# Quaternion sums as three 256-element instructions, with the memory's real part negated and the keys in another order

## The reference, cut to what matters

```python
def quat_mul(q1, q2):
    r1, i1, j1, k1 = (q1[..., 0], q1[..., 1], q1[..., 2], q1[..., 3])
    r2, i2, j2, k2 = (q2[..., 0], q2[..., 1], q2[..., 2], q2[..., 3])
    r = r1 * r2 - i1 * i2 - j1 * j2 - k1 * k2
    i = r1 * i2 + i1 * r2 + j1 * k2 - k1 * j2
    j = r1 * j2 - i1 * k2 + j1 * r2 + k1 * i2
    k = r1 * k2 + i1 * j2 - j1 * i2 + k1 * r2
    return jnp.stack([r, i, j, k], axis=-1)

keys = (x @ Wk.T + bk).reshape(B, L, N_QUAT, 4)        # 64 quaternions per token
keys = keys / jnp.maximum(norm(keys), NORM_EPS)
values = (x @ Wv.T + bv).reshape(B, L, N_QUAT, 4)
memory = jnp.cumsum(quat_mul(values, keys), axis=1)
retrieved = quat_mul(memory, quat_conj(keys)).reshape(B, L, D)
retrieved = retrieved / jnp.sqrt(positions)[None, :, None]
normed = layernorm(retrieved) * ln_g + ln_b
return x + (normed @ Wo.T + bo)
```

## Time and profile before

| | us |
|---|---|
| median of 3 runs | 720.98 |
| profiled execution | 720.35 |
| its span | 718.6 |
| busy PE | 652.3 (91%) |
| busy DVE | 613.9 (85%) |
| busy POOL | 569.9 (79%) |
| busy ACT | 414.1 (58%) |

### The profile page before, as it was taken

How to read it: one execution, slowest core, us unless ns; L and a number is a source line. 1 busy time by engine, 2 the same in 40 slices (tenths; PEclk the granted TensorE clock), 3 DMA queues, 4 the chain that set the end, 5 groups by cost and what they waited for, 6 DMA issues and landing times. The chain is left out here.

```text
span 718.6 us, 13029 instructions
## 1 busy us (share of the span) xinstructions
PE 652.3 (91%) x3536; PEld 541.8 (75%) x3536; DVE 613.9 (85%) x1378; ACT 414.1 (58%) x743; POOL 569.9 (79%) x879
## 2 busy tenths in 40 slices
PE   2999999999778988988988989989967999999997
PEld 2899998898556766766766766767756898999986
DVE  5878877765699999999999999999995877788764
ACT  4667777665435455454454454554526776677762
POOL 3788889875578888888888888888883689888873
PEclk9999999999989999999999999999988999999999
DMA  7720000000000000000000000000000011111112
GB/s 256 240 63 0 0 0 0 0 1 1 0 2 0 1 0 0 0 0 0 0 0 0 0 0 0 0 0 0 2 1 0 25 36 58 58 58 58 37 51 89
DMA packets 18442, 18.67 MB, mean 26 GB/s; under 512 B 752, under 2 KB 18160, under 8 KB 18416
## 3 DMA queue, kind: packets, MB, share of 16 engines
q1 hardware_dynamic: 18416, 18.36, 7.8%
HBM read 9.97 MB, written 8.39 MB: 26 GB/s over the span
## 5 line engine op out<-in xcount | busy, mean ns | idle before, releaser
L222 POOL TENSOR_TENSOR bhalf<-xn 128x128 f32<-128x128 f32 x256 | 118.1, 492 | 30.0 <-DVE xn L567 30.0
L1135 PE MATMUL bank<-wkv,m_xnT 128*128 128x256 f32 x512 | 134.9, 394 | 5.5 <-DVE khat L561 4.1
L1079 PE MATMUL bank<-wffn,kact 128*128 128x256 f32 x512 | 117.0, 381 | 1.6 <-DVE kact L402 1.6
L1135 PEld LDWEIGHTS bank<-wkv,m_xnT 128*128 128x128 f32 x512 | 92.2, 196 | 25.3 <-issue 4.5
L1079 PEld LDWEIGHTS bank<-wffn,kact 128*128 128x128 f32 x512 | 94.7, 190 | 13.9 <-issue 1.1
L284 POOL TENSOR_TENSOR xk_lo<-xk,xk_hi 128x1024 fp32r<-128x1024 f32 x30 | 71.0, 2368 | 31.9 <-ACT xk_hi L712 31.9
L946 POOL TENSOR_TENSOR xr_lo<-xr,xr_hi 128x1024 fp32r<-128x1024 f32 x32 | 76.2, 2381 | 18.1 <-ACT xr_hi L718 16.4
L953 POOL TENSOR_TENSOR res<-res,gating_buffers 128x1024 f32 (+1 forms) x31 | 75.4, 2433 | 9.1 <-DVE gating_buffers L409 8.6
L567 DVE TENSOR_TENSOR xn<-bank,khat 128x1024 f32<-128x1024 f32 x64 | 77.8, 1216 | 1.4
L567 DVE TENSOR_TENSOR gating_buffers<-bank,khat 128x1024 f32<-128x1024 f32 x64 | 77.6, 1212 | 0.0
L1046 PE MATMUL bank<-wffn_hi,xr_hi 128*128 128x256 f32 x256 | 71.4, 279 | 0.3 <-ACT res L819 0.3
(11 more groups left out here) (108 smaller groups left out, 1663.0 us busy)
## 6 DMA issues: line engine op xcount, KB each, us to landing
res<-x SPq DMA_DIRECT2D x16, 512.0 KB, 4.4
out<-res SPq DMA_DIRECT2D x15, 512.0 KB, 2.9
wkv<-w_kv SPq DMA_DIRECT2D x1, 512.0 KB, 7.3
out<-res SPq DMA_DIRECT2D x2, 256.0 KB, 2.2
wffn<-w_k SPq DMA_DIRECT2D x1, 256.0 KB, 3.9
wffn<-w_r SPq DMA_DIRECT2D x1, 256.0 KB, 4.1
wffn<-w_v SPq DMA_DIRECT2D x1, 256.0 KB, 4.6
wo<-w_o SPq DMA_DIRECT2D x1, 256.0 KB, 6.6
```

What stands on the lines that cost most here:

```text
L222: last = engine.tensor_tensor(o, a, b, op)
L1079: last = nc.tensor.matmul(dst[:, i, :], x[:, f, i * P:(i + 1) * P], wffn[:, w, f, :], start=f == 0, stop=f == FC - 1)
L1135: nc.tensor.matmul(dst[:, i, :], m_xnT[:, f, i * P:(i + 1) * P], wkv[:, f, col:col + D], start=f == 0, stop=False)
```

## The change

The real part of `memory` and of `bound` is kept negated, and the keys have their last two components exchanged (real, i, k, j). With values (real, i, j, k) the binding gives components in the order -real, j, k, i. In each of the two quaternion products every output component is then one product less another, plus the sum of two products. So the first half is one subtraction over 256 elements, the second half one addition over 256, and the total one addition over 256. The four products that an instruction takes lie at regular distances in two directions; `picked` builds that access pattern, in part with negative steps.

The exchange of key components is made on the device: `wkv` is loaded in four DMAs instead of one, and the bias row in `bias3` is written in four copies instead of one. Host and engines of each operation are as before. PE waits for all four DMAs.

```diff
+BIND_PLUS, BIND_MINUS, BIND_REST = (5, 3, 12, 10), (0, 6, 9, 15), ((11, 8, 7, 4), (14, 13, 2, 1))
+RET_PLUS, RET_MINUS, RET_REST = (13, 1, 14, 2), (0, 6, 9, 15), ((7, 12, 3, 8), (10, 11, 4, 5))
+
+def picked(products, slots):
+    a, b, c, d = slots
+    assert a + d == b + c
+    n = products.shape[-1]
+    first = products[:, a, :]
+    return bass.AP(tensor=first.tensor, offset=first.offset,
+                   ap=[list(first.ap[0]), [(c - a) * n, 2], [(b - a) * n, 2], [1, n]])
...
         def bind_halves(engine, j, b, i):
             s = 2 * j + b
             engine.wait_ge(bprod_done[i], s + 1)
             need(engine, bound_done[i], s)
-            p, ha, hq = bprod[:, i, :, :], bhalf[:, i, 0, :, :], bhalf[:, i, 1, :, :]
-            additions(engine,
-                   [(ha[:, 0:3:2, :], p[:, 0:3:2, :], p[:, 5:8:2, :], ALU.subtract),
-                    (ha[:, 1:4:2, :], p[:, 1:4:2, :], p[:, 4:7:2, :], ALU.add),
-                    (hq[:, 0:3:2, :], p[:, 10:14:3, :], p[:, 15:7:-7, :], ALU.add),
-                    (hq[:, 1:4:2, :], p[:, 11:13:1, :], p[:, 14:8:-5, :], ALU.subtract)],
-                   bhalf_done[i])
+            p = bprod[:, i, :, :]
+            engine.tensor_tensor(quarters(bhalf[:, i, 0, :]), picked(p, BIND_PLUS), picked(p, BIND_MINUS), ALU.subtract)
+            engine.tensor_tensor(quarters(bhalf[:, i, 1, :]), picked(p, BIND_REST[0]), picked(p, BIND_REST[1]),
+                                 ALU.add).then_inc(bhalf_done[i], 1)
...
-            out4 = bound[:, b, i, :].rearrange("p (c n) -> p c n", n=Q)
-            additions(engine,
-                   [(out4[:, 0:1, :], ha[:, 0:1, :], hq[:, 0:1, :], ALU.subtract),
-                    (out4[:, 1:4, :], ha[:, 1:4, :], hq[:, 1:4, :], ALU.add)],
-                   bound_done[i])
+            engine.tensor_tensor(bound[:, b, i, :], bhalf[:, i, 0, :], bhalf[:, i, 1, :], ALU.add).then_inc(bound_done[i], 1)
...
         def ret_halves(engine, j, b, i):
-            additions(engine,
-                   [(ha[:, 0:1, :], p[:, 0:1, :], p[:, 5:6, :], ALU.add),
-                    (ha[:, 1:4, :], p[:, 4:13:4, :], p[:, 1:4, :], ALU.subtract),
-                    (hq[:, 0:1, :], p[:, 10:11, :], p[:, 15:16, :], ALU.add),
-                    (hq[:, 1:4:2, :], p[:, 14:8:-5, :], p[:, 11:5:-5, :], ALU.subtract),
-                    (hq[:, 2:3, :], p[:, 7:8, :], p[:, 13:14, :], ALU.subtract)],
-                   rhalf_done[i])
+            p = rprod[:, i, :, :]
+            engine.tensor_tensor(quarters(rhalf[:, i, 0, :]), picked(p, RET_PLUS), picked(p, RET_MINUS), ALU.subtract)
+            engine.tensor_tensor(quarters(rhalf[:, i, 1, :]), picked(p, RET_REST[0]), picked(p, RET_REST[1]),
+                                 ALU.add).then_inc(rhalf_done[i], 1)
...
-            sp.dma_start(wkv[:, :, :], w_kv.rearrange("(f p) n -> p f n", p=P)).then_inc(wkv_in, 16)
+            sp.dma_start(wkv[:, :, 0:2 * Q], w_kv_rows[:, :, 0:2 * Q]).then_inc(wkv_in, 16)
+            sp.dma_start(wkv[:, :, 2 * Q:3 * Q], w_kv_rows[:, :, 3 * Q:4 * Q]).then_inc(wkv_in, 16)
+            sp.dma_start(wkv[:, :, 3 * Q:4 * Q], w_kv_rows[:, :, 2 * Q:3 * Q]).then_inc(wkv_in, 16)
+            sp.dma_start(wkv[:, :, D:], w_kv_rows[:, :, D:]).then_inc(wkv_in, 16)
...
-            nc.scalar.copy(bias3[:, :], v_flat[:, 0:3 * D]).then_inc(bias_rows_ready, 1)
+            nc.scalar.copy(bias3[:, 0:2 * Q], v_flat[:, 0:2 * Q])
+            nc.scalar.copy(bias3[:, 2 * Q:3 * Q], v_flat[:, 3 * Q:4 * Q])
+            nc.scalar.copy(bias3[:, 3 * Q:4 * Q], v_flat[:, 2 * Q:3 * Q])
+            nc.scalar.copy(bias3[:, D:], v_flat[:, D:3 * D]).then_inc(bias_rows_ready, 1)
```

More of the change, by code:

```diff
@@ L143, in macaron @@
         rprod = gating_buffers[:, :, :].rearrange("p i (c n) -> p i c n", n=Q)
-        bhalf = sb("bhalf", [P, 2, 2, 4, Q])
-        rhalf = sb("rhalf", [P, 2, 2, 4, Q])
+        bhalf = sb("bhalf", [P, 2, 2, D])
+        rhalf = sb("rhalf", [P, 2, 2, D])
         bound = kact[:, :, :].rearrange("p b (t n) -> p b t n", n=D)
@@ L217, in macaron, with quarters @@
         block = ctx.enter_context(nc.Block())
[L220 to L223, removed]
+        def quarters(ap):
+            return ap.rearrange("p (y x n) -> p y x n", y=2, x=2)
         def bind_sum(engine, j, b, i):
@@ L246, in bind_total @@
             need(engine, after_done[i], s - 1)
-            ha, hq = bhalf[:, i, 0, :, :], bhalf[:, i, 1, :, :]
-            out4 = bound[:, b, i, :].rearrange("p (c n) -> p c n", n=Q)
-            additions(engine,
-                   [(out4[:, 0:1, :], ha[:, 0:1, :], hq[:, 0:1, :], ALU.subtract),
-                    (out4[:, 1:4, :], ha[:, 1:4, :], hq[:, 1:4, :], ALU.add)],
-                   bound_done[i])
+            engine.tensor_tensor(bound[:, b, i, :], bhalf[:, i, 0, :], bhalf[:, i, 1, :], ALU.add).then_inc(bound_done[i], 1)
         def ret_sum(engine, j, b, i):
@@ L263, in ret_halves @@
             need(engine, ret_done[i], s)
-            p, ha, hq = rprod[:, i, :, :], rhalf[:, i, 0, :, :], rhalf[:, i, 1, :, :]
-            additions(engine,
-                   [(ha[:, 0:1, :], p[:, 0:1, :], p[:, 5:6, :], ALU.add),
-                    (ha[:, 1:4, :], p[:, 4:13:4, :], p[:, 1:4, :], ALU.subtract),
-                    (hq[:, 0:1, :], p[:, 10:11, :], p[:, 15:16, :], ALU.add),
-                    (hq[:, 1:4:2, :], p[:, 14:8:-5, :], p[:, 11:5:-5, :], ALU.subtract),
-                    (hq[:, 2:3, :], p[:, 7:8, :], p[:, 13:14, :], ALU.subtract)],
-                   rhalf_done[i])
+            p = rprod[:, i, :, :]
+            engine.tensor_tensor(quarters(rhalf[:, i, 0, :]), picked(p, RET_PLUS), picked(p, RET_MINUS), ALU.subtract)
+            engine.tensor_tensor(quarters(rhalf[:, i, 1, :]), picked(p, RET_REST[0]), picked(p, RET_REST[1]),
+                                 ALU.add).then_inc(rhalf_done[i], 1)
         def ret_total(engine, j, b, i):
@@ L276, in ret_total @@
             need(engine, m["normed_done"], s - 1)
-            additions(engine, [(ret[:, b, i, :], rhalf[:, i, 0, :, :].rearrange("p c n -> p (c n)"),
-                                rhalf[:, i, 1, :, :].rearrange("p c n -> p (c n)"), ALU.add)], ret_done[i])
+            engine.tensor_tensor(ret[:, b, i, :], rhalf[:, i, 0, :], rhalf[:, i, 1, :], ALU.add).then_inc(ret_done[i], 1)
         def key_low(engine, ops, e, j, b):
@@ L298, in _ @@
             sp.dma_start(wo[:, :, :], w_o.rearrange("(f p) n -> p f n", p=P)).then_inc(wo_in, 16)
-            sp.dma_start(wkv[:, :, :], w_kv.rearrange("(f p) n -> p f n", p=P)).then_inc(wkv_in, 16)
+            w_kv_rows = w_kv.rearrange("(f p) n -> p f n", p=P)
+            sp.dma_start(wkv[:, :, 0:2 * Q], w_kv_rows[:, :, 0:2 * Q]).then_inc(wkv_in, 16)
+            sp.dma_start(wkv[:, :, 2 * Q:3 * Q], w_kv_rows[:, :, 3 * Q:4 * Q]).then_inc(wkv_in, 16)
+            sp.dma_start(wkv[:, :, 3 * Q:4 * Q], w_kv_rows[:, :, 2 * Q:3 * Q]).then_inc(wkv_in, 16)
+            sp.dma_start(wkv[:, :, D:], w_kv_rows[:, :, D:]).then_inc(wkv_in, 16)
             with sp.Fori(1, NJ) as j:
@@ L1187, in output @@
                     last.then_inc(m["O_done"], 1)
-                pe.wait_ge(wkv_in, 16)
+                pe.wait_ge(wkv_in, 16 * 4)
                 pe.wait_ge(mem_ready, 1)
```

## The result

| | before | after |
|---|---|---|
| median of 20 runs, us | 720.99 | 722.79 |
| lowest and highest | 719.86, 723.36 | 721.24, 723.86 |
| profiled execution, us | 720.35 | 723.8 |
| busy DVE, us | 613.9 | 616.7 |
| busy POOL, us | 569.9 | 531.8 |

The ratio of the times is 1.0020, with a 95% interval of 1.0012 to 1.0028. The changed kernel is slower by 1.4 us if the means of the 20 runs are compared (721.19 and 722.62; this is what the ratio says), and by 1.8 us by the medians. POOL has 38 us less of busy time and DVE, with fewer and longer instructions, 3 us more.

The account below looks back on a forecast made before the run. The memory stage was taken to go at DVE's pace, much of it waiting for POOL; +4.0 us in steady rounds less 0.6 in the last two made +3.4, so 724.4 us, range 711 to 726.6.

Parts of the forecast that it names:

- The exchange of turns: Memory stage: DVE and POOL sums with both operands in SBUF run one at a time, each waiting for the other.
- 25 rounds of +0.16, +4.0 us: Steady memory rounds: first half to product takes 3.06 us against 2.90, 0.16 more in each of 25 rounds.
- The walk: Steady round, step by step from DVE's first half to the product, POOL's second ksum going first: 3.06 us.
- The last two rounds, -0.6: End of memory stage, no ksum: last round -0.2 us undisturbed, the one before -0.4 us.
- The start, 0: Kernel start: extra bias copies and DMA issues hide in slack, taken as 0; at most 2 us if uncovered.
- In the first three rounds PE's late projections set the pace, 0: First three memory rounds: PE's late projections set the pace, so the change there counts 0.
- the rival's order: DVE's first half runs unhindered ahead of POOL's second ksum; 2.55 us to the product, -0.35 per round; chance 0.20.
- the law of the exchange: DVE and POOL sums: how long after the partner's end a waiting sum ends, e.g. DVE 0.28, POOL 0.59 at 256 elements.
- DVE first: Rival, steady rounds: DVE's first half precedes POOL's second ksum, -0.35 us per round, 711.6 us; chance 0.20.
- Fewer waits, each as long: Rival, DVE's halves: five become two, waits as long as now, -0.9 us per round, 698 us; chance 0.07.
- Alternation: Rival, the loop's two-round body: DVE-first and POOL-first rounds cancel, 720 to 722 us; chance 0.08.
- the second rival: DVE's halves: fewer waits, each as long as now, halves near 0.41 us both, 698 us; chance 0.07.

Follow-up runs that it names:

- ksum_late: Changed kernel plus a POOL memset of 256 elements every round, delaying the second key sum: 710.18 us, 0.9849 of before.
- all_small: Changed kernel's component order, DMAs and bias copies, but short sums on both POOL and DVE: 719.57 us, 0.9978 of before.
- after_again: The changed kernel run and profiled once more, no edit: 722.96 us, 1.0028 of before.
- dve_small: Changed kernel with DVE's sums cut into five short pieces, POOL's kept at 256: 735.52 us, 1.0206 of before.
- pool_small: Changed kernel with POOL's sums cut into short pieces, DVE's halves kept at 256: 697.82 us, 0.9682 of before.
- pool_small_late: Changed kernel with short POOL sums, long DVE halves and a POOL memset ahead of the second key sum: 691.97 us, 0.9605 of before.

## Why the prediction was right in kind and too high in size

- **The exchange of turns: right.** Forecast halves of 0.64 and 0.94 us, n_var 0.68, knorm 0.54, POOL's total 0.87, ksum 0.46; measured 0.66, 0.96, 0.69, 0.53, 0.86 (at 425.80) and 0.45. The second key sum was 0.07 ahead of DVE's half, of 0.10 forecast. The Trainium skill ("SBUF — State Buffer", "Who interferes with whom") has whoever issues first keep the port for its instruction, and ksum_late, which changes only who is first, agrees with that by its 12.8 us. Two rows, at 225.39 and at 342.22, speak against it at first sight; they are told of at the end.
- **25 rounds of +0.16, +4.0 us: right, a little low.** Measured +0.18 per round, +4.37 over the 24 rounds between the marks. The walk had 3.06 from half to product, this round 3.09 and the mean 3.08; POOL ends 0.59 to 0.61 behind DVE, where I took 0.59 each time.
- **The last two rounds, -0.6: right, in part by luck.** -0.51 in the mean, -0.59 in the first pair of executions. The sum leaves two of the 32 rounds out, the two ahead of the last two. Between half and product they changed by +0.18 and -0.21 us in the first pair, so that the gap doesn't show. In the last but one I had -0.4; half to product went from 2.59 us (529.10 to 531.69) to 2.21:

```profile
532.68 0.39 DVE L271 TENSOR_TENSOR rhalf<-gating_buffers 128x256 f32<-128x256 f32 x1
532.99 0.95 DVE L272 TENSOR_TENSOR rhalf<-gating_buffers 128x256 f32<-128x256 f32 x1
...
534.89 1.22 DVE L572 TENSOR_TENSOR gating_buffers<-bank,khat 128x1024 f32<-128x1024 f32 x1
```

- **The start, 0: right.** The bias copy of 0.80 became four that end 0.99 after they began (21.99 to 22.98); the unit keys of the first round of the stage came at 188.79 instead of 188.64, and all_small, which has the same start, is not slower than before.
- **"In the first three rounds PE's late projections set the pace, 0": this step failed.** It should have been about -1.2, and with it the sum would have been +2.2; the spans differ by 2.1 us, the means of 20 runs by 1.4. It is the one term of the sum whose reason the traces contradict. In the first round PE did not set the pace at all. Before, DVE is busy for 11.40 of its 11.81 us and PE for 8.40 (first line below). In after_again, to which the other two lines belong, DVE is busy for 17.78 of the 18 us from 200 to 218, and PE for 11.41, at the full granted clock.

```profile
202.13:213.94 11.81, 8.40 (x29) 5.60 (x29) 11.40 (x27) 3.18 (x7) 9.58 (x21) 0.71 0.01 3
...
200.00:218.00 18.00, 11.41 (x55) 7.88 (x53) 17.78 (x39) 6.22 (x15) 14.74 (x20) 1.00 0.00 1
218.40:221.70 3.30, 3.30 (x11) 2.53 (x9) 3.21 (x5) 1.57 (x3) 2.16 (x3) 0.50 0.00 0
```

  What happened there is to be seen in the two timelines. Before, the five halves of the first round took 2.57 us in all, against 1.89 in the fifth; after, 1.26 from 201.97 to 203.23. The first of each fence is of the first round, the others of the second and fifth (before), of the second (after):

```profile
202.13 2.57 DVE L222 TENSOR_TENSOR rhalf<-gating_buffers 128x64 f32<-128x64 f32 x5
...
213.94 0.93 DVE L222 TENSOR_TENSOR rhalf<-gating_buffers 128x64 f32<-128x64 f32 x5
...
246.82 1.89 DVE L222 TENSOR_TENSOR rhalf<-gating_buffers 128x64 f32<-128x64 f32 x5
```

```profile
201.97 0.39 DVE L271 TENSOR_TENSOR rhalf<-gating_buffers 128x256 f32<-128x256 f32 x1
202.28 0.95 DVE L272 TENSOR_TENSOR rhalf<-gating_buffers 128x256 f32<-128x256 f32 x1
...
212.76 0.40 DVE L271 TENSOR_TENSOR rhalf<-gating_buffers 128x256 f32<-128x256 f32 x1
213.07 0.42 DVE L272 TENSOR_TENSOR rhalf<-gating_buffers 128x256 f32<-128x256 f32 x1
```

  In the first round DVE's halves met not the second but the first key sum and what follows. With five pieces DVE had to let pass both key sums and more; with two, half one went first and the halves waited for one sum only. From half to product it was 3.78 us before and 2.53 after; 0.2 of this is lost again behind the product, where n_gain takes 0.38 us. That is the rival's order, here in the first round in all three executions. The other kernels bear out that DVE's lengths decide here: the first round lasts 11.40 us in all_small and 11.80 in dve_small, with short pieces on DVE, and 10.56 in pool_small, with long ones. The earlier trace rows has half of it: the first key sum at 202.48 beside the sum at 202.53. I used that row for the law of the exchange and did not walk its round through.

  In the second and third rounds the claim is half right. In the second the halves are undisturbed in both kernels where the key sum comes late (POOL idle 2.20 us before a ksum at 213.97, until ACT's squares, which had waited for PE). Which round that is differs: in after_again it is the third, with a half of 0.39, and there PE had run in the window before at a granted clock of 0.50, the lower level of 1.2 GHz, fully busy (3.30 of 3.30 us, last line above) after it had been idle for some 6.6 of 18 us. What these stretches give or take is not separated from chance: 0.2 us for rounds two to four together, in the mean of the executions, against a spread of 0.7 in one round.

- **The rivals.** DVE first: wrong for the steady rounds, and right to 0.03 us for what that order costs. Fewer waits, each as long: wrong, for the waits grew; half one waits 0.25 us and half two 0.55. Alternation: there is none, DVE's first half takes 0.64 to 0.67 us in all 24 rounds of the loop, though their lengths alternate between 11.05 and 11.14. They alternate alike before (10.87 and 10.96), behind the product. The fast kernels, pool_small and pool_small_late, are another thing than the second rival: they have the fewer waits of DVE's long sums and keep the short ones of POOL.

What stays open: the 0.7 us ahead of h0, and why all_small is 1.1 us faster than before (0.7 of it is the 0.03 us per round in the loop, which lies between half and product).

## What to carry to other kernels

When two engines take turns at their operands, as DVE and POOL do here, each wait is as long as the partner's instruction. So try few and long instructions on the engine that sets the pace and short ones on its partner: here the same sums took 697.8 us that way round and 735.5 the other. Then look which of the two asks first at the place where they meet; a tenth of a microsecond there was worth 12.8 us. And walk the odd rounds at the ends of a loop through by their own rows, as the steady one: their order of turns can be the other.

## What the runs showed of the hardware that was not expected

- A start in the trace does not seem always to be a claim. In the first round after, POOL's key sum starts at 201.92 and DVE's half at 201.97, yet the half goes first (0.39 us) and the key sum ends 0.59 after it, at 202.95. The sum before on POOL was still running until 201.97; the key sum is recorded as started under it, and the other two executions show the same:

```profile
201.24 0.73 POOL L259 TENSOR_TENSOR kact<-bhalf 128x256 f32<-128x256 f32 x1
201.92 1.03 POOL L990 TENSOR_TENSOR ksum<-ksq 128x256 f32<-128x256 f32 x1
```

  Where a semaphore stands between, as before the second key sum, a lead of 0.07 us is enough (423.50 to 423.57).
- The turn need not change after one instruction. In pool_small_late ksum asked at 342.22, under half one, and half two passed ahead of it, as sums did in the earlier trace rows at 225.39; in ksum_late ksum asked at 340.65, under half one too, and went next; in the changed kernel's steady rounds POOL and DVE took strict turns. The two kernels with the memset would fit the point above: POOL's memset ends at 342.27 in the one, after half two's start of 342.23, and at 340.70 in the other, before half two's 340.91. The row at 225.39 doesn't fit it, for there ksum came after an idle time and still three sums passed. What decides is not settled.
